# Pairing the row-maximum matmuls of attention over row halves, and running the first expert stage as one stream over its batches, in a four-stage kernel on one core

## The reference, cut to what matters

```
# stage 1, x is (4, 512, 256), 16 heads of 16, 4 key/value heads
scores = einsum('bhqd,bhkd->bhqk', rope(q), rope(k)) / 4
p_g = softmax(where(causal, scores, -inf))
p_l = softmax(where(local,  scores, -inf))      # windows of 32
out = 0.5 * (p_g @ v + p_l @ v);  x = layernorm(x + out @ wo)
# stage 2, 8 experts with a hidden width of 128, 2 chosen for each token, and a shared one
gates = softmax over the 2 largest of (x @ gate_w), zero elsewhere
routed = sum_e gates[e] * (gelu(x @ w1[e] + b1[e]) @ w2[e] + b2[e])
x = layernorm(x + routed + gelu(x @ shared_w1 + shared_b1) @ shared_w2 + shared_b2)
```

## Time and profile before

| | us |
|---|---|
| runs (median, lowest, highest of 3) | 2114.64, 2112.45, 2114.76 |
| the profiled execution: its own time | 2113.24 |
| its span, first to last instruction | 2111.6 |
| PE busy in the span | 1671.7 (79%) |
| DVE, ACT, POOL busy | 1039.3, 659.0, 683.6 |
| attention stage, start to the next stage's first instruction | 0 to 600.1 |
| first expert stage | 600.1 to 838.6 |

### The profile page before, as it was taken

One profiled execution on the slowest core, in us unless ns is written; L12 is line 12 of the kernel. 1 busy time (PEld: TensorE's weight loads), 2 busy tenths in 40 slices (PEclk: granted clock), 3 DMA queues, 4 the chain that ended last, 5 costly groups with the idle time before them and its releaser, 6 DMA issues. The chain is left out here.

```text
span 2111.6 us, 28929 instructions
## 1 busy us (share of the span) xinstructions
PE 1671.7 (79%) x10666; PEld 1071.2 (51%) x10666; DVE 1039.3 (49%) x2374; ACT 659.0 (31%) x1167; POOL 683.6 (32%) x1092
## 2 busy tenths in 40 slices
PE   4797887887948886858799999999999962777771
PEld 3343444444425554423566666666666752545651
DVE  3745445454213333555367666666766421334623
ACT  3151331522311211545244454444445210111010
POOL 2020200200000000015767777777777711000152
PEclk8999798999968888989899999999999765898596
DMA  1000000000020001430121222222122113110173
GB/s 45 1 2 1 20 1 1 21 1 11 1 71 20 20 20 36 132 65 15 36 51 28 43 41 41 51 51 49 28 46 33 28 26 99 55 65 30 33 165 105
DMA packets 216824, 83.93 MB, mean 40 GB/s; under 512 B 166249, under 2 KB 211666, under 8 KB 216706
## 3 DMA queue, kind: packets, MB, share of 16 engines
q1 hardware_dynamic: 205266, 67.90, 14.5%
q0 software_dynamic: 5376, 12.59, 2.4%
q10 hardware_dynamic: 6064, 1.86, 0.4%
HBM read 50.60 MB, written 31.72 MB: 39 GB/s over the span
## 5 line engine op out<-in xcount | busy, mean ns | idle before, releaser
L1717 DVE SCALAR_TENSOR_TENSOR d_conv<-d_prep,k_cw,d_conv 128x511 f32<-128x511 f32 (+2 forms) x288 | 214.2, 746 | 32.7 <-ACT d_conv L1548 26.0
L1669 POOL TENSOR_TENSOR d_prod<-d_blk 64x30 f32<-64x30 f32 (+4 forms) x360 | 173.6, 482 | 102.0 <-DMA d_blk<-mid_a_blk 74.8
L1334 PE MATMUL d_prep<-k_hT,k_w 128*128 128x512 f32 x384 | 187.9, 614 | 21.6 <-POOL d_power L1643 12.4
L1673 POOL TENSOR_TENSOR d_blk<-d_blk,d_prod 64x30 f32<-64x30 f32 (+4 forms) x360 | 184.3, 512 | 28.2
L419 ACT ACTIVATE a_probs<-a_acc 128x896 f32<-128x896 f32 x128 | 117.4, 917 | 219.6 <-PE a_acc L244 131.8
L516 DVE TENSOR_REDUCE a_top<-a_turn 128x4 f32<-128x512 f32 (+3 forms) x240 | 147.3, 652 | 62.4 <-PE a_turn L207 54.3
L465 POOL TENSOR_TENSOR a_rstd<-a_rstd,a_mhalf 128x4 f32<-128x4 f32 x4 | 4.1, 1027 | 407.9 <-DVE a_rstd L565 407.9
L1334 PEld LDWEIGHTS d_prep<-k_hT,k_w 128*128 128x128 f32 x384 | 68.0, 197 | 82.1 <-issue 48.1
L1373 PE MATMUL d_prep<-d_kq 128*128 128x256 f32 x384 | 95.5, 393 | 15.1 <-DVE d_qkT L1749 15.1
L1548 ACT ACTIVATE d_conv<-d_prep,k_cw 128x512 f32<-128x512 f32 x96 | 65.9, 687 | 130.4 <-PE d_prep L1334 130.1
L1373 PEld LDWEIGHTS d_prep<-d_kq 128*128 128x128 f32 x384 | 73.4, 198 | 44.4 <-DVE d_qkT L1749 26.9
(11 more groups left out here) (352 smaller groups left out, 3687.7 us busy)
## 6 DMA issues: line engine op xcount, KB each, us to landing
mid_gate<-p_gate SPq DMA_DIRECT2D x4, 768.0 KB, 3.4
mid_v<-p_v_tok SPq DMA_DIRECT2D x4, 768.0 KB, 3.5
d_v_h<-mid_v SPq DMA_DIRECT2D x12, 256.0 KB, 5.6
d_gate_h<-mid_gate SPq DMA_DIRECT2D x12, 256.0 KB, 5.5
mid_a_blk<-d_AT SPq DMA_DIRECT2D x48, 64.0 KB, 2.0
d_blk<-mid_a_blk SPq DMA_DIRECT2D x12, 256.0 KB, 3.5
mid_u_blk<-d_blk SPq DMA_DIRECT2D x12, 256.0 KB, 2.9
mid_l_blk<-d_blkT SPq DMA_DIRECT2D x12, 256.0 KB, 3.7
```

The costliest lines, as they stand in the source:

```text
L1334: last = nc.tensor.matmul(PB[f % 2][:], w[:, n % 2, i, k, :], hT[:, k, b * T:(b + 1) * T], start=k == 0, stop=k == CK - 1)
L1669: nc.gpsimd.tensor_tensor(pr, blk[:, 0:t, t:t + 1].broadcast_to([lanes, t, m]), blk[:, t:t + 1, t + 1:BLK].broadcast_to([lanes, t, m]), AL ...
L1673: nc.gpsimd.tensor_tensor(blk[:, 0:t, t + 1:BLK], blk[:, 0:t, t + 1:BLK], pr, ALU.subtract).then_inc(subst, 1)
L1717: ins = nc.vector.scalar_tensor_tensor(dst, PB[f % 2][:, 0:T - j], cw[:, n % 2, f % 2, TAPS - 1 - j:TAPS - j], dst, ALU.mult, ALU.add)
```

## The change

In attention, `sel` and `ntopT` exist twice, on the partitions 0 to 47 and 64 to 111. `split_tops` writes each part for both halves in one instruction with twice the elements. `score` issues the 48-row matmuls of both banks first, `a0`'s from the lower row half and `a1`'s from the upper, and then everything over 128 rows. One more load of `sel` (192 KB) and one memset of `nparts` come with it.

In the expert stage, SP loads the identity and x of batch 0 first, then what the routing needs, then w1, then w2, and there are semaphores for each of the three. `x`, `xT`, `gates` and `y` are double. The loop is written out, and the turning, routing and gate transposing of batch b + 1 stand between the projections of batch b; the first two `hide` of b + 1 stand where batch b has none left. On ACT and DVE the corresponding copies, the exponential, `choose` (top 2), `weigh` and the normalisation of the batch before follow the same scheme. Everything behind this stage is the same code.

```diff
-        sel = sb("sel", [3 * A_HEADS, A_HEADS, P], BF16)
+        sel = sb("sel", [P, A_HEADS, P], BF16)
...
-        nparts = sb("nparts", [P, 2, NT, A_HEADS, 3], BF16)
-        ntopT = sb("ntopT", [3 * A_HEADS, 2, T], BF16)
+        nparts = sb("nparts", [P, 2, NT, 2, H_ROWS], BF16)
+        ntopT = sb("ntopT", [P, 2, T], BF16)
...
-                             (qmask[:], d["c_qmask"]), (kmask[:], d["c_kmask"]), (sel[:], d["c_sel"]),
...
+                             (qmask[:], d["c_qmask"]), (kmask[:], d["c_kmask"]), (sel[0:3 * A_HEADS, :, :], d["c_sel"]), (sel[H_ROWS:H_ROWS + 3 * A_HEADS, :, :], d["c_sel"]),
...
                 a0, a1 = AB[u][:, 0, :], AB[u][:, 1, :]
+                lo, hi = slice(0, 3 * A_HEADS), slice(H_ROWS, H_ROWS + 3 * A_HEADS)
                 if u == 0:
-                    nc.tensor.matmul(a0, sel[:, h, :], ntopT[:, 1, :], start=True, stop=False)
+                    nc.tensor.matmul(a0, sel[lo, h, :], ntopT[lo, 1, :], start=True, stop=False)
+                    nc.tensor.matmul(a1[:, 0:256], sel[hi, h, :], ntopT[hi, 0, 256:512], start=True, stop=False)
+                    nc.tensor.matmul(a1[:, 256:384], sel[hi, h, :], ntopT[hi, 0, 384:512], start=False, stop=False)
                     for i in range(NT):
                         s = window_start(i)
                         nc.tensor.matmul(a0[:, i * P:(i + 1) * P], kg[:, s:s + P], qh[:, i * P:(i + 1) * P],
                                          start=False, stop=False)
                     nc.tensor.matmul(a0, identb[:], kmask[:, 1:5, :].rearrange("p a q -> p (a q)"), start=False, stop=True)
-                    nc.tensor.matmul(a1[:, 0:256], sel[:, h, :], ntopT[:, 0, 256:512], start=True, stop=False)
-                    nc.tensor.matmul(a1[:, 256:384], sel[:, h, :], ntopT[:, 0, 384:512], start=False, stop=False)
                     nc.tensor.matmul(a1[:, 0:256], kg[:, 256:384], qh[:, 256:512], start=False, stop=False)
                     nc.tensor.matmul(a1[:, 256:384], kg[:, 384:512], qh[:, 384:512], start=False, stop=False)
                     nc.tensor.matmul(a1[:, 0:128], identb[:], kmask[:, 0, :], start=False, stop=False)
                     last = nc.tensor.matmul(a1[:, 256:384], identb[:], kmask[:, 0, :], start=False, stop=True)
                 else:
+                    for j, a, r in ((0, a0, lo), (1, a1, hi)):
+                        nc.tensor.matmul(a[:, 0:T - P * j], sel[r, h, :], ntopT[r, 0, P * j:T], start=True, stop=False)
                     for j, a in ((0, a0), (1, a1)):
                         w = T - P * j
-                        nc.tensor.matmul(a[:, 0:w], sel[:, h, :], ntopT[:, 0, P * j:T], start=True, stop=False)
                         nc.tensor.matmul(a[:, 0:w], kg[:, P * j:P * (j + 1)], qh[:, P * j:T], start=False, stop=False)
                         last = nc.tensor.matmul(a[:, 0:P], identb[:], kmask[:, 0, :], start=False, stop=True)
                 last.then_inc(rescored, 1)
...
+                both = nparts[:, :, :, :, 0:3 * A_HEADS].rearrange("p g t d (h s) -> p (g t) d h s", s=3)
+                one = nparts[:, :, :, 0, 0:3 * A_HEADS].rearrange("p g t (h s) -> p g t h s", s=3)
+                wide = lambda t: t[:].rearrange("p g t h -> p (g t) h")[:, :, None, :].broadcast_to([P, 2 * NT, 2, A_HEADS])
                 link(nc.vector.tensor_scalar(ntop[:], top[:], -1.0, None, ALU.mult))
-                link(nc.vector.tensor_copy(nparts[:, :, :, :, 0], ntop[:]))
-                link(nc.vector.tensor_tensor(nrest[:], ntop[:], nparts[:, :, :, :, 0], ALU.subtract))
-                link(nc.vector.tensor_copy(nparts[:, :, :, :, 1], nrest[:]))
-                link(nc.vector.tensor_tensor(nrest[:], nrest[:], nparts[:, :, :, :, 1], ALU.subtract))
-                nc.vector.tensor_copy(nparts[:, :, :, :, 2], nrest[:]).then_inc(nsplit, 1)
+                link(nc.vector.tensor_copy(both[:, :, :, :, 0], wide(ntop)))
+                link(nc.vector.tensor_tensor(nrest[:], ntop[:], one[:, :, :, :, 0], ALU.subtract))
+                link(nc.vector.tensor_copy(both[:, :, :, :, 1], wide(nrest)))
+                link(nc.vector.tensor_tensor(nrest[:], nrest[:], one[:, :, :, :, 1], ALU.subtract))
+                nc.vector.tensor_copy(both[:, :, :, :, 2], wide(nrest)).then_inc(nsplit, 1)
...
+            def load_x(b):
+                if b >= 2:
+                    sp.wait_ge(added, F_SUMS * (b - 2) + 1)
+                    sp.sem_inc(carrier_sp)
+                sp.dma_start(x[:, b % 2, :, :], x1_b[b, :, :, :]).then_inc(x_in[b % 2], 16)
+
+            sp.dma_start(ident[:], d["c_ident"]).then_inc(first_in, 16)
+            load_x(0)
+            sp.dma_start(w_gate[:], d["L0_ffn_gate_w"].rearrange("(k p) n -> p k n", p=P)).then_inc(first_in, 16)
             for k in range(CK):
-                loads += [(w1[:, k, 0:F_SH, :], d["L0_ffn_shared_w1"][k * P:(k + 1) * P, :].rearrange("p (e n) -> p e n", e=F_SH)),
-                          (w1[:, k, F_SH:, :], d["L0_ffn_w1"][:, k * P:(k + 1) * P, :].rearrange("e p n -> p e n"))]
-            for dst, src in loads:
...
+            for k in range(CK):
+                sp.dma_start(w1[:, k, F_SH:, :], d["L0_ffn_w1"][:, k * P:(k + 1) * P, :].rearrange("e p n -> p e n")).then_inc(w1_in, 16)
+            for dst, src in ((b2[0:F_E, :], d["L0_ffn_b2"]), (b2[F_E:F_E + 1, :], d["L0_ffn_shared_b2"].rearrange("(a n) -> a n", a=1)),
+                             (w2[:, 0:F_SH, :], d["L0_ffn_shared_w2"].rearrange("(k p) n -> p k n", p=P)),
+                             (w2[:, F_SH:, :], d["L0_ffn_w2"].rearrange("e p n -> p e n"))):
+                sp.dma_start(dst, src).then_inc(w2_in, 16)
+            for b in range(1, BATCH):
+                load_x(b)
...
+            turn_x(0)
+            route(0)
+            hide(0, 0)
+            hide(0, 1)
+            for b in range(BATCH):
+                hide(b, F_SH)
+                if b == 0:
+                    turn_gates(0)
                 for u in range(F_SUMS):
                     if F_SH + 1 + u < F_UNITS:
-                        hide(F_SH + 1 + u)
-                    project(u)
+                        hide(b, F_SH + 1 + u)
+                    elif b + 1 < BATCH:
+                        hide(b + 1, F_SH + 1 + u - F_UNITS)
+                    project(b, u)
+                    if b + 1 < BATCH:
+                        if u == 2:
+                            turn_x(b + 1)
+                        if u == 3:
+                            route(b + 1)
+                        if u == 7:
+                            turn_gates(b + 1)
...
+            keep_x(0)
+            raise_gates(0)
+            act.wait_ge(w1_in, 16 * 6)
+            for b in range(BATCH):
+                    if n == (1 if b else F_SH + 1):
+                        keep_gates(b)
+                    gelu(b, n)
+                    if b + 1 < BATCH:
+                        if n == 5:
+                            keep_x(b + 1)
+                        if n == 8:
+                            raise_gates(b + 1)
...
+            choose(0)
+            weigh(0)
+            for b in range(BATCH):
+                for u in range(F_SUMS):
+                    add(b, u)
+                    if u == 1 and b:
+                        normalise(b - 1)
+                    if b + 1 < BATCH:
+                        if u == 3:
+                            choose(b + 1)
+                        if u == 5:
+                            weigh(b + 1)
+                measure(b)
+            normalise(BATCH - 1)
```

More of the change, by code:

```diff
@@ L472, in _ @@
         def _(dve):
-            dve.wait_ge(loaded, 160)
+            dve.wait_ge(loaded, 176)
+            dve.wait_ge(ones, 4)
             count = [0]
@@ L734, in _, with turn_gates, hide @@
-                for n in range(F_SH + 1):
-                    hide(n)
+            def turn_gates(b):
                 pe.wait_ge(gated, b + 1)
                 for t in range(NT):
-                    last = nc.tensor.transpose(TB[1][0:F_E + 1, t * P:(t + 1) * P], gates[:, t, :], ident[:])
+                    last = nc.tensor.transpose(TB[1][0:F_E + 1, t * P:(t + 1) * P], gates[:, b % 2, t, :], ident[:])
                 last.then_inc(g_turned, 1)
-                pe.wait_ge(gT_ready, b + 1)
+            def hide(b, n):
+                unit = F_UNITS * b + n
+                if unit == 0:
+                    pe.wait_ge(w1_in, 16 * 6)
+                if unit >= 2:
+                    pe.wait_ge(gelued, unit - 1)
+                for k in range(CK):
+                    last = nc.tensor.matmul(HB[unit % 2][:], w1[:, k, n, :], xT[:, b % 2, k, :], start=k == 0, stop=k == CK - 1)
+                last.then_inc(hidden, 1)
@@ new lines, in project @@
+            def project(b, u):
+                chunks = range(F_SH) if u == 0 else [u + F_SH - 1]
+                total_u = F_SUMS * b + u
+                if total_u == 0:
+                    pe.wait_ge(w2_in, 16 * 4)
+                if u == 0:
```

(17 more changed lines are left out.)

144 lines of the change are left out of this document (68 added, 76 removed).

## The result

| | before | changed |
|---|---|---|
| runs, median (lowest to highest), us | 2114.70 (2112.45 to 2117.82) | 2013.61 (2009.29 to 2014.03) |
| span of the profiled execution | 2111.6 | 2012.1 |
| attention stage | 600.1 | 552.5 |
| first expert stage | 238.5 | 187.1 |
| all that follows | 1273.0 | 1272.5 |

Four runs each; the ratio of the changed kernel to the one before is 0.9519, with a 95% interval of 0.9507 to 0.953. The forecast was 2040.7 with a range down to 2031. The direction and the places were right, and the gain of 101 us is larger than the 74 forecast and than the range allowed: the attention stage gave 47.6 us where 32.0 were forecast, the expert stage 51.4 where it was 41.9.

A forecast was written before the change was run, and what follows sets the result against it. PE was taken as the engine others wait for in attention, and as standing idle between expert batches. 2113.2 - 32.0 (pairs) - 8.9 (start) - 33.0 (boundaries) = 2039.3, plus 1.4 for the runs' median: 2040.7 us, range 2031 to 2055.

The forecast's parts named there:

- The pairs' price: Attention: each unit gets 0.35 us shorter, 0.18 from two fewer row-count changes and 0.17 from overlap; 44.8 us over 128 units.
- The deductions: Attention: places where PE waits for something else and the pairs' gain is lost, 10.6 us off 44.8.
- ACT in heads 2 to 5: Attention, three batches: PE would gain 3.15 us before head 6's `turn_stack`, but ACT allows only 1.35; 5.4 us lost.
- `mix` behind heads 9 and 13: Attention, three batches: unit 0 there covers DVE's `mix`, so PE would wait the gain away; 2.1 us lost.
- Last batch, heads 0 to 3: Attention, only scores there: one tile's round of 2.80 us would shrink to 2.45, PE alone needing 2.10; 1.4 us lost.
- Heads 6 to 8: Attention: these heads wait in part for ACT's copies; 1.0 us lost, judged by eye.
- Casts and load: Attention: casts of twice the elements cost 1.7 us and the extra load at the start delays x by 0.5 us.
- The start: Start of the expert stage: x is issued 8.9 us earlier and all of it is gained, with 7.5 as the other end.
- The boundaries: Between expert batches: 23.3 us plus a 0.4 wait, less 12.65 of remaining PE work, gains 11.1 each; 33.0 taken for three.
- No overlap: Rival, chance 0.12: the pair's matmuls run one behind the other and only row-count changes are saved in attention; 2055 us.
- A clock that drops inside the stream: Rival, chance 0.12: in the expert stage the clock drops for a few us behind the logits in three batches; 2047 to 2053.
- ACT ending more waits: Rival, chance 0.06: ACT also ends the wait in all of attention heads 6 to 8, about 3 x 2.1 us lost; 2046.

The follow-up runs named there:

- experiment 4: The changed kernel with both 48-row matmuls of a unit still side by side but both from the lower row half: 2031.4 us, ratio 0.9614.
- experiment 5: The changed kernel with both row halves in use but each 48-row matmul back in its old place in the unit: 2063.0 us, ratio 0.976.
- Experiment 2: The changed kernel's attention (the pairs) with the expert loop of the kernel before: 2068.9 us, ratio 0.9785 to the kernel before.
- experiment 8: The changed kernel with the expert stage's x of batch 0 issued after all weights, as before: 2023.1 us, ratio 0.9572.
- Experiments 6: The kernel before with 12 unused matmuls after each batch's last project in the expert loop and 2 ahead of the logits: 2115.8 us, ratio 1.0003.
- experiment 7: The kernel before with 6 unused matmuls after each batch's last project in the expert loop and 1 ahead of the logits: 2102.6 us, ratio 0.9945.

## Why the forecast fell short

**The pairs' price: right.** 0.37 us measured, 0.35 forecast, 0.21 of it for two changes of row count and 0.16 for the hidden columns (experiment 4). Over 128 units this is 47.4, not 44.8: 2.6 us. "Tiles of one array do run at once there, so I take the lower end" was right. Against the Trainium skill's 3.07x for four row tiles ("TensorE: Matmul & The Clock Gate", Part 3, Measured speedup) I had put an estimate of 0.02 us a pair; the rows show 0.00. The same section's span model, 4 ns for each further tile, is the one that fits.

**The deductions: too large.** The forecast took off 10.6 us and the traces show 6.3.
- ACT in heads 2 to 5: 5.4 forecast, 2.8 found (2.3 at head 6 and 0.5 at head 2). The step that failed is "of ACT's 2.0 us of gaps I keep 0.65": ACT has 0.2 us of gaps left now and PE waits 1.14 us at head 6, so ACT is the bound there, but I had let it keep idle time that it gave up. From head 2's start to `turn_stack` of head 6 it is 16.4 us for 18.8, a gain of 2.4 where I had said 1.4.
- x in batches 1 and 2: 0.7 and 0.7. `mix` behind heads 9 and 13: 2.1 and 2.2. Both right.
- Last batch, heads 0 to 3: 1.4 and 0.6. I had read "one tile's round is 2.80 us" off two starts of PE. That was PE's own work. The tile's round ended sooner: 513.54 + 0.92 is 514.46, 0.26 before the next start. 2.54 - 0.37 gives 2.17, and 2.22 was measured.
- Heads 6 to 8: "1.0 us by eye" was nothing. These heads got 0.74 each, all but the wait at head 6.

**Casts and load: right.** 2.2 forecast, 1.7 by experiment 5; a cast of 256 elements takes 0.38 us.

**Clock in the attention: not in the sum at all.** 47.4 - 6.3 - 1.7 = 39.4, and the means of several profiles differ by 44.9; the one pair of profiles by 47.6. In the old order, head 1 of batch 1 had its projections at the lower clock, in the new one not. The old head first, then the new, and last the old head 1 of batch 0, which had the full clock:

```profile
238.69:247.92 9.23, 9.23 (x36) 5.06 (x35) 2.85 (x8) 3.96 (x7) 0.00 (x0) 0.65 0.09 31
```
```profile
224.80:231.38 6.58, 5.79 (x35) 3.64 (x34) 2.34 (x6) 3.85 (x7) 0.00 (x0) 0.99 0.21 73
```
```profile
96.41:103.36 6.95, 6.48 (x36) 3.72 (x35) 2.71 (x8) 3.85 (x7) 0.00 (x0) 1.00 0.00 0
```

In the five old profiles head 1 of batches 0 to 2 had a granted clock of 0.63 to 0.77 in 13 of 15 cases and took 7.87 to 9.45 us; in the two others it took 6.95 and 6.96. In the three new ones it took 6.58 or 6.59 in all nine. Three old ones together are 26.0 us on the mean, so 26.0 - 3 x 6.95 = 5.1 us were the low clock, which the new order doesn't pay. The pairs give this head 0.37 and not 0.74, since PE now waits 0.79 us in it for ACT's copy of the turned x, for 0.5 (the group L177 above). That leaves 5.1 - 3 x 0.37 = 4.0 of the missing 5.5; the other 1.5 lie in head 0 and the tails, where stretches of low clock differ from profile to profile, and I don't place them. Experiment 2's profile has the same head at 0.85 and also 6.58 us long: a low clock ahead of that wait took its place (PE doesn't wait for the copy there). Why the low stretch reached into head 1 in the old order, and doesn't in the new, is open; no run tested it by itself.

**The start: 8.9 forecast, 9.4 in experiment 8.** Right, w1 was early.

**The boundaries: the step that failed most.** "What PE must still do of it: turn x, 1.8, logits 3.45." I took both from the rows of the old boundary, and these ran at 1.2 GHz, which the earlier trace rows said (0.71 over the boundary). In the stream they take 0.87 and 1.70. This is 2.7 us a boundary, 8.0 in three, nearly all of the 9.5 us by which the stage beat the forecast, and more than any other term of the sum missed by. I had corrected the hides to the full clock and left the turn and logits as they were. Experiments 6 and 7 show the cause in the old loop itself: with PE kept at work the same two steps cost 0.9 and 1.7 to 1.8, and with little enough filling the kernel gains 10.5 us.

**The rivals.** No overlap: refuted by experiment 4. A clock that drops inside the stream: the granted clock was 1.00 from 570 to 730, behind each of the logits too. The rival wasn't empty: in the old loop of experiment 7, where waits of 0.65 and 0.31 us stood around the turn, it did drop behind the logits at two of three boundaries. ACT ending more waits: it ends one a batch and four short ones in the last, as above. The sum of the misses is 2.6 + 4.3 + 0.5 (casts and load) + 5.5 + 2.7 (that one profile against the means) in the attention and 9.5 in the expert stage: 25.1 of the 27.1 us; the rest lies behind these stages and within the scatter of runs.

## What to carry to other kernels

A duration read next to a stall is a duration at the clock of that place: before it enters a sum for another place, look at the granted clock of its own window and scale it. Two matmuls over few rows were worth pairing on two row halves only side by side; more than half of the gain here (0.21 of 0.37 us a unit), all of it that needs no second copy, is fewer changes of row count. A tile's round is the sum of its own steps up to the release, not the distance of two starts of the engine that is busy.
